# Attention softmax of a decoder layer: causal mask added by VectorE together with the row maximum, probability scale applied in two places, high half read in two halves

## The chip, the cores and the metric

One NeuronCore of a Trainium2 chip runs the whole decoder layer in one launch. The metric is device time in microseconds (us), from one launch to its end. The kernel before was timed three times: 1171.23 us is the median, 1167.91 and 1172.15 us are the ends. Engines: TensorE (PE) multiplies matrices into PSUM banks, VectorE (DVE), ScalarE (ACT) and GpSimd (POOL) work elementwise, SyncE (SP) issues DMAs. Each engine takes its own instructions in the order in which they are written; semaphores connect them.

## The reference, cut to what matters

A pre-norm decoder layer on `x` (4 x 512 x 512): latent attention with 16 heads and a causal mask, then an int8-like quantised linear layer pair, then a mixture of 8 experts with the best 2 per token. The change touches the attention's softmax alone.

```python
q = rmsnorm(x @ w_qa, q_norm_w) @ w_qb            # 16 heads, 128 plain + 64 rotary
kv = x @ w_kva                                    # 128 latent + 64 rotary (shared by the heads)
k_nope, v = split(rmsnorm(kv_c, kv_norm_w) @ w_kvb)
q_rope, k_rope = rotated by position (cos, sin)
scores = einsum('blhd,bmhd->bhlm', q, k) / sqrt(192)
scores = where(tril, scores, -1e30)
attn = softmax(scores, axis=-1)
out = einsum('bhlm,bmhd->blhd', attn, v).reshape(B, L, 2048) @ w_o
x = x + out                                       # x here went through a layer norm first
x = x + quantised_linear_pair(layernorm(x))       # scaled and rounded to +-127, silu gate between
x = x + mixture_of_experts(layernorm(x))
```

## The kernel before, in words

Everything that must be exact beyond fp16 is kept as two fp16 halves, a high one (the value rounded) and a low one (the rest), and a product of two such numbers is three matmuls (`TRI`).

After a preparation of the weights, `walk` goes over 32 steps `i`, each a pair of heads of one batch (4 batches x 8 pairs). All engines run the same `walk` with their own `pair` function; `j` is `i & 1`, so even and odd steps have different tables of extra work. In a step there are 8 slots `g`: two heads with four row blocks `k = g & 3` of 128 query rows, whose causal width is `n = 128 (k + 1)` columns. `G = 8 i + g` counts row blocks over the whole walk: 256 of them, 64 of each width (128, 256, 384, 512).

One row block passes these stations:

- PE `scores` (L1898 to L1903): five matmuls of width `n` into one of three score banks, and a sixth, 128 columns wide, which adds the mask (identity times `maskb`, with -1e30 above the diagonal) to the last 128 columns.
- DVE `row_max` (L1512): a reduction over the bank that gives the negated row maximum `NEGM`.
- POOL `bias` (L1059): `NB = NEGM * sc_exp`, one value a row.
- ACT `exps` (L1218): `exp(sc_exp * s + NB)` from the bank into `PF` in SBUF, with the row sum.
- DVE `row_scale`: the reciprocal of the sum (L1519) and its product with 4096, `R4` (L1521). `probs_hi` (L1529): the high half, `PF * R4` in fp16. `probs_lo` (L1536): the low half, `PF * R4` minus the high half.
- SP `turn_probs` (L1012): a DMA transposes both halves into `PT` (semaphore `pt_in[k]`). PE `values` (L1915) multiplies them with the latents once all four blocks of a head have landed.

DVE's `pair` issues in slot `g` first `row_max(g)` and then `row_scale`, `probs_hi` and `probs_lo` of `g - 1`. PE may be three row blocks ahead, since there are three score banks (`s_exp`).

Beside this, each step prepares the rotary part of the next one. PE `rope_mm(i+1)` (L1859, in even steps slot 4) is copied by ACT `rope_swap` in four pieces (L1237), POOL multiplies it with the sines (`rope_sin`, L1064), DVE multiplies the original with the cosines (`rotate`, L1556), POOL adds (`rope_sum`, L1070) and subtracts (`rope_split`, L1075), and ACT makes the halves (L1245, L1249). Even steps up to 22, twelve of them, also prepare one tile of the next batch (`prep`): ACT L1192 and L1194 (squares, after PE L1828), DVE L1474 and following, POOL `prep_norm` (L1053), and DVE `prep_split` (a cast L1495 and a subtraction L1497), on which PE `prep_t2` (L1837) waits in slot 6. The four even steps 24 to 30 have no such tile. Odd steps up to 21 do the layer norm of a tile ahead (DVE L1439 to L1449, POOL `prep_rstd` L1049). `nope_mm` (L1880) and `project` (L1930) are the other matmuls of a step.

In POOL's `pair`, slot `g` is `bias(g)` and then that slot's rotary part: in even steps `rope_sin` in slot 3, `rope_sum` in slot 5, `rope_split` in slot 6. `rope_sin` waits for `r_swap`, which ACT raises.

Of the kernel before, what the change touches and what calls it, by code (L numbers as in the profile page):

```python
# [17 lines left out]
B, L, D = 4, 512, 512  # L18
# [17 lines left out]
def decoder_layer(nc, x, fside, ctxw, w_qa, q_norm_w, w_qb, w_kva, kv_norm_w, w_kvb, w_o,  # L36
# [16 lines left out]
    with es:  # L53
# [3 lines left out]
        identf = es.enter_context(nc.sbuf_tensor("identf", [P, P], fp32))  # L57
        maskb = es.enter_context(nc.sbuf_tensor("maskb", [P, P], bf16))
        scal = es.enter_context(nc.sbuf_tensor("scal", [P, 40], fp32))
# [13 lines left out]
        qnw, knw = scal[:, 34:37], scal[:, 37:38]  # L73
        amaxq = scal[:, 31:34]

        ARENA = 52400
# [55 lines left out]
        small = take(40)  # L132
        NEGM, NB, SUM, RC, R4 = (small[:, 20 + 4 * k:24 + 4 * k] for k in range(5))
        rstd = small[:, 10:11]
# [122 lines left out]
        def ph_part(k, hl):  # L257

            return ph(k).rearrange("p (t l c) -> p t l c", l=2, c=P)[:, :, hl, :]
# [771 lines left out]
        def _(pool):  # L1031
            pool.memset(half, -0.5).then_inc(const_made, 1)
            pool.memset(phalf, 0.5).then_inc(const_made, 1)
            pool.memset(eone, math.e).then_inc(const_made, 1)
            for t, fill in ((ident16, 1.0), (identb, 1.0), (identf, 1.0)):
                pool.memset(t[:, :], 0.0).then_inc(const_made, 1)
            pool.memset(maskb[:, :], 0.0).then_inc(const_made, 1)
            pool.memset(KN[:, P + DR:2 * P + DR], 0.0).then_inc(const_made, 1)
            pool.wait_ge(const_made, 8)
            for t in (ident16, identb, identf):  # L1040
                pool.affine_select(out=t[:, :], in_=t[:, :], compare_op=ALU.not_equal, fill=1.0, base=0,
                                   pattern=[[-1, P]], channel_multiplier=1).then_inc(const_made, 1)

            pool.affine_select(out=maskb[:, :], in_=maskb[:, :], compare_op=ALU.is_ge, fill=-1e30, base=0,
                               pattern=[[-1, P]], channel_multiplier=1).then_inc(const_made, 1)
# [9 lines left out]
            def bias(G, g):  # L1055

                pool.wait_ge(s_max, G + 1)
                k = g & 3
                pool.tensor_tensor(NB[:, k:k + 1], NEGM[:, k:k + 1], sc_exp, ALU.mult).then_inc(s_bias, 1)  # L1059

# [16 lines left out]
            def pair(i, j, first=False, last=False, prep=None, ahead=None):  # L1077
                G = 8 * i
                for g in range(8):
                    bias(G + g, g)  # L1080
                    if (j, g) == (0, 2):
                        if prep is not None:
                            prep_norm(prep[0])
# [52 lines left out]
            rope_split(0, 0)  # L1136
            walk(pair)
            later_pool(pool)

# [223 lines left out]
        def _(dve):  # L1363
# [25 lines left out]
            def units_of_heads():  # L1389

                dve.wait_ge(amax_all, 2)
                own(dve.tensor_scalar(amx[:, 3:5], amx[:, 3:5], 1e-30, None, ALU.max))
                own(dve.reciprocal(ainv[:, 3:5], amx[:, 3:5]))
                own(dve.tensor_scalar(sc_exp, uk, amx[:, 3:4], 1.0 / math.sqrt(DN + DR), ALU.mult, ALU.mult))
                dve.tensor_scalar(sc_y, amx[:, 2:3], amx[:, 4:5], 1.0 / PSCALE, ALU.mult, ALU.mult).then_inc(units, 1)

# [111 lines left out]
            def row_max(G, g):  # L1508

                n = ((g & 3) + 1) * P  # L1510
                dve.wait_ge(s_mm, G + 1)
                dve.tensor_reduce(NEGM[:, (g & 3):(g & 3) + 1], banks[S_BANKS[G % 3]][:, 0:n], AX.X, ALU.max,  # L1512
                                  negate=True).then_inc(s_max, 1)

            def row_scale(G, g):

                k = g & 3
                dve.wait_ge(s_exp, G + 1)
                dve.reciprocal(RC[:, k:k + 1], SUM[:, k:k + 1]).then_inc(s_rc, 1)  # L1519
                dve.wait_ge(s_rc, G + 1)  # L1520
                dve.tensor_scalar(R4[:, k:k + 1], RC[:, k:k + 1], PSCALE, None, ALU.mult).then_inc(s_r4, 1)  # L1521

            def probs_hi(i, g):

                k, G = g & 3, 8 * i + g
                dve.wait_ge(s_r4, G + 1)
                if not (i == 0 and g < 4):
                    dve.wait_ge(pt_in[k], 16 * (2 * i + (g >> 2)))
                dve.tensor_scalar(ph_part(k, 0), pf(k).rearrange("p (t c) -> p t c", c=P), R4[:, k:k + 1], None,  # L1529
                                  ALU.mult).then_inc(s_hi, 1)  # L1530

            def probs_lo(G, g):

                k = g & 3
                dve.wait_ge(s_hi, G + 1)
                dve.scalar_tensor_tensor(out=ph_part(k, 1), in0=pf(k).rearrange("p (t c) -> p t c", c=P),  # L1536
                                         scalar=R4[:, k:k + 1], in1=ph_part(k, 0), op0=ALU.mult,
                                         op1=ALU.subtract).then_inc(s_lo, 1)
# [239 lines left out]
        def _(pe):  # L1778


            pe.wait_ge(const_made, 12)

# [103 lines left out]
            def scores(i, j, g):  # L1886
# [14 lines left out]
                pe.matmul(bank[:, 0:n], qr(j, h, q, P), kr(bp, 0, 0, n), start=False, stop=False)  # L1901
                pe.matmul(bank[:, 0:n], qr(j, 2, q, P), kr(bp, 1 + h, 0, n), start=False, stop=False)  # L1902
                pe.matmul(bank[:, q:n], identb[:, :], maskb[:, :], start=False, stop=True).then_inc(s_mm, 1)  # L1903

# [180 lines left out]
```

## Time and profile before

| what | before |
|---|---|
| device time, median of 3 (ends) | 1171.23 us (1167.91 to 1172.15) |
| span of the profiled execution | 1169.4 us |
| time around the span | not shown for this execution; the median lies 1.8 us above the span |
| PE busy | 980.4 us, 84% |
| DVE busy | 959.2 us, 82% |
| ACT busy | 678.1 us, 58% |
| POOL busy | 296.4 us, 25% |

The span is the time from the first to the last instruction. The walk lies at about 162 to 880 us; before it the weights are prepared, after it come the two later layers. Between 300 and 850 us the walk runs at the full clock of TensorE and repeats itself every two steps. The busy time of an engine adds its instructions' records; records of neighbours overlap a little, on PE a lot, so that for PE the distance from one start to the next is the cost of an instruction, not its own length.

### The profile page before, as it was taken

The page shows a single profiled execution, that of the slowest core. Times are in us where ns is not written, and L with a number is a line of the kernel's source. Part 1 is how long each engine was busy: PE and PEld are TensorE (multiplying, and loading weights), DVE is VectorE, ACT ScalarE, POOL GpSimd, SP SyncE. Part 2 cuts the span into 40 slices and gives each one's busy share as a digit, 9 for nine tenths or more (in the row PEclk, how much of TensorE's full clock was granted, in tenths as well). Part 3 has the DMA queues.
Part 4 walks back from the last instruction along what each step waited for, and adds up shares of the span by engine and source line. Part 5 has one row for each costly group of instructions (what it writes and reads, how often), then busy time and mean ns, then how long its engine had stood idle before and what let it go on. Part 6 is the DMA issues. An engine that isn't in the chain of part 4 may idle for free.

```text
span 1169.4 us, 18715 instructions
## 1 busy us (share of the span) xinstructions
PE 980.4 (84%) x6106; PEld 574.0 (49%) x6124; DVE 959.2 (82%) x2669; ACT 678.1 (58%) x1449; POOL 296.4 (25%) x524
## 2 busy tenths in 40 slices
PE   0446667899999999999999999999978655559997
PEld 0234444555555555555555555555545544435553
DVE  5757749989989888989998988888868898866885
ACT  1446557667667666756666666656512676754442
POOL 1036533223223223222322222213100113221211
PEclk9769779999999999999999999999989888769999
DMA  9300003433323336334335244336363520001333
GB/s 350 139 1 1 1 8 73 75 59 71 71 59 67 66 62 142 62 64 69 65 68 138 55 68 60 64 67 140 68 218 86 168 91 19 0 1 36 84 80 91
DMA packets 217328, 90.78 MB, mean 78 GB/s; under 512 B 191496, under 2 KB 202760, under 8 KB 216720
## 3 DMA queue, kind: packets, MB, share of 16 engines
q1 hardware_dynamic: 217232, 89.58, 33.5%
q8 instruction: 50, 0.82, 0.3%
q14 instruction: 46, 0.38, 0.1%
HBM read 36.06 MB, written 7.34 MB: 37 GB/s over the span
## 4 chain that ended last, share of the span: by engine, by line
PE 53%; DVE 30%; ACT 6%; issue 5%; POOL 3%; DMA 3%; SPq 0%; DVEq 0%; ACTq 0%; POOLq 0%
PE bank L1930 13%; PE bank L1880 8%; PE bank L1915 6%; PE bank L1828 3%; PE bank L1859 3%; DVE arena L709 2%; PE bank L1898 2%; DVE arena L711 2%; PE bank L1901 2%; PE bank L1899 2%; PE bank L1900 2%; PE bank L1902 2%; DVE arena L791 2%; DVE arena L675 2%; DVE arena L1529 2%
## 5 line engine op out<-in xcount | busy, mean ns | idle before, releaser
L1218 ACT ACTIVATE arena<-bank,arena,scal 128x128 f32<-128x128 f32 (+3 forms) x256 | 157.7, 616 | 112.7 <-POOL arena L1059 111.6
L1930 PE MATMUL bank<-arena 128*128 128x512 f16 x768 | 179.1, 381 | 1.9 <-DVE arena L1562 1.9
L1536 DVE SCALAR_TENSOR_TENSOR arena<-arena 128x128 f16<-128x128 f32 (+3 forms) x256 | 142.2, 555 | 9.1
L1059 POOL TENSOR_TENSOR arena<-arena,scal 128x1 f32<-128x1 f32 x256 | 51.7, 203 | 347.4 <-DVE arena L1512 345.7
L1880 PE MATMUL bank<-arena 128*128 128x512 f16 x576 | 137.6, 385 | 0.0
L1529 DVE TENSOR_SCALAR arena<-arena 128x128 f16<-128x128 f32 (+3 forms) x256 | 125.4, 490 | 7.4 <-DVE arena L1521 0.8
L1512 DVE TENSOR_REDUCE arena<-bank 128x1 f32<-128x128 f32 (+3 forms) x256 | 123.7, 483 | 7.8 <-PE bank L1903 6.7
L1915 PE MATMUL bank<-arena 128*128 128x512 f16 (+3 forms) x768 | 117.7, 304 | 11.5 <-DMA arena<-arena 5.8
L1930 PEld LDWEIGHTS bank<-arena 128*128 128x128 f16 x768 | 72.9, 98 | 81.0 <-issue 4.4
L1915 PEld LDWEIGHTS bank<-arena 128*128 128x128 f16 x768 | 71.8, 99 | 63.0 <-issue 16.5
L1237 ACT ACTIVATE arena<-bank 32x512 f32<-32x512 f32 x128 | 75.3, 588 | 26.0 <-PE bank L1859 24.7
L1898 PE MATMUL bank<-arena 128*128 128x128 f16 (+3 forms) x256 | 77.0, 301 | 9.1 <-DVE arena L1429 5.0
L1880 PEld LDWEIGHTS bank<-arena 128*128 128x128 f16 x576 | 54.4, 99 | 55.8 <-issue 3.5
L1249 ACT ACTIVATE arena<-arena 64x512 f16<-64x512 f32 x128 | 79.9, 624 | 1.2
L1902 PE MATMUL bank<-arena 128*128 128x128 f16 (+3 forms) x256 | 76.9, 300 | 0.0
L1900 PE MATMUL bank<-arena 128*128 128x128 f16 (+3 forms) x256 | 76.9, 300 | 0.0
L1901 PE MATMUL bank<-arena 128*128 128x128 f16 (+3 forms) x256 | 76.9, 300 | 0.0
L1899 PE MATMUL bank<-arena 128*128 128x128 f16 (+3 forms) x256 | 76.9, 300 | 0.0
L1228 ACT ACTIVATE arena<-bank 128x512 f16<-128x512 f32 x64 | 38.2, 596 | 65.8 <-PE bank L1880 65.5
L835 PE MATMUL bank<-identf,arena 128*128 128x128 f32 x192 | 37.7, 355 | 40.8 <-DVE arena L721 35.9
L1828 PE MATMUL bank<-arena 128*128 128x384 f16 (+1 forms) x384 | 54.8, 303 | 18.1 <-DVE arena L1386 15.7
L1064 POOL TENSOR_TENSOR arena<-arena 128x512 f32<-128x512 f32 x32 | 44.9, 1404 | 94.2 <-ACT arena L1237 94.1
(201 smaller groups left out, 2049.5 us busy)
## 6 DMA issues: line engine op xcount, KB each, us to landing
arena<-in_L_attn_w_qb SPq DMA_DIRECT2D x1, 4608.0 KB, 21.6
arena<-arena SPq DMA_TRANSPOSE x272, 2.7
arena<-in_x SPq DMA_DIRECT2D x4, 1024.0 KB, 6.9
arena<-in_L_attn_w_o SPq DMA_DIRECT2D x1, 4096.0 KB, 31.9
arena<-in_fside_BxS2xS SPq DMA_DIRECT2D x4, 1024.0 KB, 8.8
arena<-in_L_ffn_w SPq DMA_DIRECT2D x8, 512.0 KB, 7.6
out<-arena SPq DMA_DIRECT2D x16, 256.0 KB, 2.3
arena<-in_x SPq DMA_DIRECT2D x12, 256.0 KB, 3.0
```

The source lines that it names most:

```text
L1218: act.activation(pf(k), banks[S_BANKS[G % 3]][:, 0:n], ACT.Exp, bias=NB[:, k:k + 1], scale=sc_exp, accum_out=SUM[:, k:k + 1]).then_inc(s_e ...
L1512: dve.tensor_reduce(NEGM[:, (g & 3):(g & 3) + 1], banks[S_BANKS[G % 3]][:, 0:n], AX.X, ALU.max, negate=True).then_inc(s_max, 1)
L1529: dve.tensor_scalar(ph_part(k, 0), pf(k).rearrange("p (t c) -> p t c", c=P), R4[:, k:k + 1], None, ALU.mult).then_inc(s_hi, 1)
L1536: dve.scalar_tensor_tensor(out=ph_part(k, 1), in0=pf(k).rearrange("p (t c) -> p t c", c=P), scalar=R4[:, k:k + 1], in1=ph_part(k, 0), op0= ...
L1880: last = pe.matmul(banks[Q_BANK][:, :], wq(a, c, (i & 7) * 2 + h), ct(bp, b, c, 0, L), start=(k == 0), stop=(k == 3 * QC - 1))
L1898: pe.matmul(bank[:, 0:n], qn(h, 0, q, P), ct(bp, 0, QC, 0, n), start=True, stop=False)
L1899: pe.matmul(bank[:, 0:n], qn(h, 0, q, P), ct(bp, 1, QC, 0, n), start=False, stop=False)
L1900: pe.matmul(bank[:, 0:n], qn(h, 1, q, P), ct(bp, 0, QC, 0, n), start=False, stop=False)
L1901: pe.matmul(bank[:, 0:n], qr(j, h, q, P), kr(bp, 0, 0, n), start=False, stop=False)
L1902: pe.matmul(bank[:, 0:n], qr(j, 2, q, P), kr(bp, 1 + h, 0, n), start=False, stop=False)
L1915: last = pe.matmul(banks[O_BANK][:, kt * P:L], cn(bp, a, kt), pt(h, b, kt, kt * P, L - kt * P), start=(kt == 0 and n == 0), stop=(kt == TB ...
L1930: last = pe.matmul(banks[Y_BANK][:, :], ot(gp, a, k, (q & 3) * P, P), wo(b, gp * GH + k), start=(k == 0 and n == 0), stop=(k == GH - 1 and ...
```

## The change: mask, scale and halves

1. The mask matmul (L1903) is gone, and the fifth matmul ends the group. The mask is now `maskw`, 512 columns wide, zero except for the last 128. `row_max` is one `tensor_tensor_reduce` on DVE: it reads the bank and the last `n` columns of `maskw`, writes the sum back into the bank and gives the row maximum `ROWM`, not negated. The program has two instructions for it, the operation over the tile and one that writes the 128 x 1 result.
2. `bias` multiplies with `nsc_exp`, the negated `sc_exp` (one more small DVE instruction before the walk).
3. `row_scale` is the reciprocal alone. `probs_hi` takes the reciprocal as first scalar and 4096 as second. `R4`, which only `probs_lo` still reads, is made by POOL in a new function `row_unit`, placed right behind the next row block's `bias`; `probs_lo` waits for it (`s_r4`).
4. `probs_hi` reads and writes its columns as two halves of 64 in each block of 128 (`halves`), so the outermost size is 2 for each width.

```diff
@@ POOL, before the walk @@
-            pool.memset(maskb[:, :], 0.0).then_inc(const_made, 1)
+            pool.memset(maskw[:, :], 0.0).then_inc(const_made, 1)
-            pool.affine_select(out=maskb[:, :], in_=maskb[:, :], compare_op=ALU.is_ge, fill=-1e30, base=0,
+            pool.affine_select(out=maskw[:, L - P:L], in_=maskw[:, L - P:L], compare_op=ALU.is_ge, fill=-1e30, base=0,
                                pattern=[[-1, P]], channel_multiplier=1).then_inc(const_made, 1)
@@ POOL @@
-                pool.tensor_tensor(NB[:, k:k + 1], NEGM[:, k:k + 1], sc_exp, ALU.mult).then_inc(s_bias, 1)
+                pool.tensor_tensor(NB[:, k:k + 1], ROWM[:, k:k + 1], nsc_exp, ALU.mult).then_inc(s_bias, 1)
+
+            def row_unit(G, g):
+
+                k = g & 3
+                pool.wait_ge(s_rc, G + 1)
+                if G >= 4:
+                    pool.wait_ge(s_lo, G - 3)
+                pool.tensor_tensor(R4[:, k:k + 1], RC[:, k:k + 1], pscale, ALU.mult).then_inc(s_r4, 1)
@@ POOL, pair @@
                     bias(G + g, g)
+                    if not (first and g == 0):
+                        row_unit(G + g - 1, g - 1)
                     if (j, g) == (0, 2):
@@ DVE @@
-                dve.tensor_reduce(NEGM[:, (g & 3):(g & 3) + 1], banks[S_BANKS[G % 3]][:, 0:n], AX.X, ALU.max,
-                                  negate=True).then_inc(s_max, 1)
+                s = banks[S_BANKS[G % 3]][:, 0:n]
+                dve.tensor_tensor_reduce(out=s, in0=s, in1=maskw[:, L - n:L], scale=1.0, scalar=-3e38, op0=ALU.add,
+                                         op1=ALU.max, accum_out=ROWM[:, (g & 3):(g & 3) + 1]).then_inc(s_max, 1)
                 dve.reciprocal(RC[:, k:k + 1], SUM[:, k:k + 1]).then_inc(s_rc, 1)
-                dve.wait_ge(s_rc, G + 1)
-                dve.tensor_scalar(R4[:, k:k + 1], RC[:, k:k + 1], PSCALE, None, ALU.mult).then_inc(s_r4, 1)
+            def halves(v):
+
+                return v.rearrange("p t (h c) -> p h t c", h=2)
             def probs_hi(i, g):
-                dve.wait_ge(s_r4, G + 1)
+                dve.wait_ge(s_rc, G + 1)
-                dve.tensor_scalar(ph_part(k, 0), pf(k).rearrange("p (t c) -> p t c", c=P), R4[:, k:k + 1], None,
-                                  ALU.mult).then_inc(s_hi, 1)
+                dve.tensor_scalar(halves(ph_part(k, 0)), halves(pf(k).rearrange("p (t c) -> p t c", c=P)),
+                                  RC[:, k:k + 1], PSCALE, ALU.mult, ALU.mult).then_inc(s_hi, 1)
             def probs_lo(G, g):
                 dve.wait_ge(s_hi, G + 1)
+                dve.wait_ge(s_r4, G + 1)
@@ PE @@
-                pe.matmul(bank[:, 0:n], qr(j, 2, q, P), kr(bp, 1 + h, 0, n), start=False, stop=False)
-                pe.matmul(bank[:, q:n], identb[:, :], maskb[:, :], start=False, stop=True).then_inc(s_mm, 1)
+                pe.matmul(bank[:, 0:n], qr(j, 2, q, P), kr(bp, 1 + h, 0, n), start=False, stop=True).then_inc(s_mm, 1)
```

In a program order listing the first piece is POOL in an even step with a tile to prepare, from `prep_norm` (L1053) in slot 2 to `rope_sum` (L1070) in slot 5, before the change; L1064 is `rope_sin`, L1059 is `bias`.

```order
L1053 TENSOR_TENSOR arena<-arena,scal 128x2 [waits sv_made]
L1059 TENSOR_TENSOR arena<-arena,scal 128x1 [waits s_max]
L1064 TENSOR_TENSOR arena<-arena 128x512 [waits r_swap]
L1059 TENSOR_TENSOR arena<-arena,scal 128x1 [waits s_max] x2
L1070 TENSOR_TENSOR arena<-arena 128x512 [waits r_sin,r_rot]
```

The same place after the change; L1056 is `prep_norm`, L1062 `bias`, L1070 now `row_unit`, L1075 `rope_sin`, L1081 `rope_sum`.

```order
L1056 TENSOR_TENSOR arena<-arena,scal 128x2 [waits sv_made]
L1062 TENSOR_TENSOR arena<-arena,scal 128x1 [waits s_max]
L1070 TENSOR_TENSOR arena<-arena,scal 128x1 [waits s_lo,s_rc]
L1075 TENSOR_TENSOR arena<-arena 128x512 [waits r_swap]
L1062 TENSOR_TENSOR arena<-arena,scal 128x1 [waits s_max]
L1070 TENSOR_TENSOR arena<-arena,scal 128x1 [waits s_lo,s_rc]
L1062 TENSOR_TENSOR arena<-arena,scal 128x1 [waits s_max]
L1070 TENSOR_TENSOR arena<-arena,scal 128x1 [waits s_lo,s_rc]
L1081 TENSOR_TENSOR arena<-arena 128x512 [waits r_sin,r_rot]
```

Each `bias` now has a `row_unit` behind it, and the `row_unit` of slot 4 (row block 3) stands behind `rope_sin`.

The second piece is DVE in the same step, slot 4, before the change: `row_max(4)`, the two parts of `row_scale(3)`, `probs_hi(3)`, `probs_lo(3)`, `rotate` (L1556), `prep_split` (L1495, L1497).

```order
L1512 TENSOR_REDUCE arena<-bank 128x1 [waits s_mm]
L1519 RECIPROCAL arena<-arena 128x1 [waits s_exp]
L1521 TENSOR_SCALAR arena<-arena 128x1 [waits s_rc]
L1529 TENSOR_SCALAR arena<-arena 128x4x128 [waits pt_in3,s_r4]
L1536 SCALAR_TENSOR_TENSOR arena<-arena 128x4x128 [waits s_hi]
L1556 TENSOR_TENSOR arena<-bank,arena 128x512 [waits r_swap,r_split,r_mm]
L1495 CAST arena<-arena 128x512 [waits cn_made,ct_t,cf_made]
L1497 TENSOR_TENSOR arena<-arena 128x512 [waits ch_hi]
```

After the change (L1528 `row_max` in two instructions, L1535 reciprocal, L1547 `probs_hi`, L1555 `probs_lo`, L1575 `rotate`, L1510 and L1512 `prep_split`):

```order
L1528 ISA bank,arena<-bank,maskw 128x128 [waits s_mm]
L1528 ISA arena 128x1
L1535 RECIPROCAL arena<-arena 128x1 [waits s_exp]
L1547 TENSOR_SCALAR arena<-arena 128x2x4x64 [waits pt_in3,s_rc]
L1555 SCALAR_TENSOR_TENSOR arena<-arena 128x4x128 [waits s_r4,s_hi]
L1575 TENSOR_TENSOR arena<-bank,arena 128x512 [waits r_swap,r_split,r_mm]
L1510 CAST arena<-arena 128x512 [waits cn_made,ct_t,cf_made]
L1512 TENSOR_TENSOR arena<-arena 128x512 [waits ch_hi]
```

One small instruction is gone and one has come; `probs_lo` has a second semaphore, raised by POOL, and `rotate` and `prep_split` stand behind it as before.

## Rows read from the trace of the kernel before

**Rows 1.** 300-850 us: busy PE, PEld, DVE, ACT, POOL, clock; page's chain by engine.
```profile
300.00:850.00 550.00, 545.47 (x3478) 305.24 (x3476) 485.78 (x1352) 355.06 (x811) 143.44 (x294) 1.00 0.40 77
...
PE 53%; DVE 30%; ACT 6%; issue 5%; POOL 3%; DMA 3%; SPq 0%; DVEq 0%; ACTq 0%; POOLq 0%
```
**Rows 2.** Waits of PE, 300 to 850 us: who for whom, total, times, longest.
```profile
PE bank L1837 <- DVE arena L1497: 2.5, 9, 1.0
```
**Rows 3.** Instructions of PE in time: start, length, line, shape.
```profile
404.56 0.22 PE L1898 MATMUL bank<-arena 128*128 128x128 f16 x1
...
404.84 0.22 PE L1903 MATMUL bank<-maskb,identb 128*128 128x128 bf16 x1
404.90 0.38 PE L1930 MATMUL bank<-arena 128*128 128x512 f16 x1
```
**Rows 4.** Groups of DVE by form: count, busy us, mean ns, idle before.
```profile
L1521 DVE TENSOR_SCALAR arena<-arena 128x1 f32<-128x1 f32 x256 | 39.4, 154 | 8.8
L1529 DVE TENSOR_SCALAR arena<-arena 128x384 f16<-128x384 f32 x64 | 39.1, 611 | 1.9
L1512 DVE TENSOR_REDUCE arena<-bank 128x1 f32<-128x128 f32 x64 | 18.1, 283 | 1.0 <-PE bank L1903 1.0
L1512 DVE TENSOR_REDUCE arena<-bank 128x1 f32<-128x512 f32 x64 | 43.9, 686 | 4.3 <-PE bank L1903 3.4
L721 DVE SCALAR_TENSOR_TENSOR arena<-bank,arena 128x512 f32<-128x512 f32 x32 | 22.1, 745 | 4.2 <-PE bank L876 4.0
L1416 DVE SCALAR_TENSOR_TENSOR arena<-bank,scal,arena 128x128 f16<-128x128 f32 x32 | 9.6, 341 | 0.0
L1404 DVE SCALAR_TENSOR_TENSOR arena<-arena,scal 128x512 f16<-128x512 f32 x6 | 6.0, 1057 | 0.0
```
**Rows 5.** DVE in time, end of step 11 and step 12 (even, with a tile).
```profile
416.20 0.16 DVE L1519 RECIPROCAL arena<-arena 128x1 f32<-128x1 f32 x1 [0.94 <-ACT arena L1218]
...
435.04 0.22 DVE L1474 TENSOR_TENSOR arena<-bank,arena 128x64 f32<-128x64 f32 x1 [1.26 <-ACT arena L1194]
...
439.76 0.49 DVE L1529 TENSOR_SCALAR arena<-arena 128x512 f16<-128x512 f32 x1
440.28 0.75 DVE L1536 SCALAR_TENSOR_TENSOR arena<-arena 128x512 f16<-128x512 f32 x1
...
441.55 0.90 DVE L1495 CAST arena<-arena 128x512 f16<-128x512 f32 x1
442.49 0.69 DVE L1497 TENSOR_TENSOR arena<-arena 128x512 f16<-128x512 f32 x1
```
**Rows 6.** POOL in time, step 12, slots 3 and 4.
```profile
440.51 1.65 POOL L1064 TENSOR_TENSOR arena<-arena 128x512 f32<-128x512 f32 x1 [3.78 <-ACT arena L1237]
442.13 0.37 POOL L1059 TENSOR_TENSOR arena<-arena,scal 128x1 f32<-128x1 f32 x1
```
**Rows 7.** The wait chain before L1064, and PE in step 12.
```profile
438.05 2.39 ACT L1237 ACTIVATE arena<-bank 32x512 f32<-32x512 f32 x4 [0.41 <-PE bank L1859]
...
443.24 0.62 PE L1837 MATMUL bank<-ident,arena 128*128 128x128 f16 x8 [0.18 <-DVE arena L1497]
```
**Rows 8.** DVE and POOL at once: a read of SBUF through two ports, a small multiply.
```profile
196.85 0.49 DVE L1529 TENSOR_SCALAR arena<-arena 128x512 f16<-128x512 f32 x1
...
196.94 0.45 POOL L1059 TENSOR_TENSOR arena<-arena,scal 128x1 f32<-128x1 f32 x1
```
**Rows 9.** Step 28 (even, no tile): DVE, POOL, PE in time.
```profile
789.03 0.75 DVE L1536 SCALAR_TENSOR_TENSOR arena<-arena 128x512 f16<-128x512 f32 x1
...
790.12 1.27 POOL L1064 TENSOR_TENSOR arena<-arena 128x512 f32<-128x512 f32 x1 [3.39 <-ACT arena L1237]
791.34 0.34 POOL L1059 TENSOR_TENSOR arena<-arena,scal 128x1 f32<-128x1 f32 x2
...
793.48 1.79 PE L1915 MATMUL bank<-arena 128*128 128x512 f16 x12
```
**Rows 10.** Transposes of the probabilities at 789.8 us: issue to landing.
```profile
DMA to landing us min/median/max: 3.1/3.1/3.1
```

More of the change, by code:

```diff
@@ L57, in decoder_layer @@
         identf = es.enter_context(nc.sbuf_tensor("identf", [P, P], fp32))
-        maskb = es.enter_context(nc.sbuf_tensor("maskb", [P, P], bf16))
+        maskw = es.enter_context(nc.sbuf_tensor("maskw", [P, L], bf16))
         scal = es.enter_context(nc.sbuf_tensor("scal", [P, 40], fp32))
@@ L74, in decoder_layer @@
         amaxq = scal[:, 31:34]
+        nsc_exp = scal[:, 38:39]
+        pscale = scal[:, 39:40]
         ARENA = 52400
@@ L132, in decoder_layer @@
         small = take(40)
-        NEGM, NB, SUM, RC, R4 = (small[:, 20 + 4 * k:24 + 4 * k] for k in range(5))
+        ROWM, NB, SUM, RC, R4 = (small[:, 20 + 4 * k:24 + 4 * k] for k in range(5))
         rstd = small[:, 10:11]
@@ L1034, in _ @@
             pool.memset(eone, math.e).then_inc(const_made, 1)
+            pool.memset(pscale, PSCALE).then_inc(const_made, 1)
             for t, fill in ((ident16, 1.0), (identb, 1.0), (identf, 1.0)):
                 pool.memset(t[:, :], 0.0).then_inc(const_made, 1)
-            pool.memset(maskb[:, :], 0.0).then_inc(const_made, 1)
+            pool.memset(maskw[:, :], 0.0).then_inc(const_made, 1)
             pool.memset(KN[:, P + DR:2 * P + DR], 0.0).then_inc(const_made, 1)
-            pool.wait_ge(const_made, 8)
+            pool.wait_ge(const_made, 9)
             for t in (ident16, identb, identf):
@@ L1137, in _ @@
             walk(pair)
+            row_unit(8 * NPAIR - 1, 7)
             later_pool(pool)
@@ L1394, in units_of_heads @@
                 own(dve.tensor_scalar(sc_exp, uk, amx[:, 3:4], 1.0 / math.sqrt(DN + DR), ALU.mult, ALU.mult))
+                dve.tensor_scalar(nsc_exp, uk, amx[:, 3:4], -1.0 / math.sqrt(DN + DR), ALU.mult, ALU.mult)
                 dve.tensor_scalar(sc_y, amx[:, 2:3], amx[:, 4:5], 1.0 / PSCALE, ALU.mult, ALU.mult).then_inc(units, 1)
@@ L1778, in _ @@
         def _(pe):
-            pe.wait_ge(const_made, 12)
+            pe.wait_ge(const_made, 13)
             def transpose_head(h):
```

## The prediction

> **What bounds the kernel now.** I read the stretches first, then the chain, then who waits for whom, then single steps of the walk in order of time. From 300 to 850 us TensorE is busy 545.5 of 550 us at the full clock, VectorE 485.8 of 550 [rows 1]; more than half of the chain that ended last is TensorE's [rows 1]. In that stretch the longest entry of TensorE's waits is 2.5 us in total, for `prep_split` on VectorE [rows 2]. So the walk goes at TensorE's pace and repeats every two steps, and a matmul that goes is time gained, unless something else then comes late. VectorE is the next to look at: over two steps (44.65 us) it has pauses of 2.9 us in all beyond the usual gaps, the two long ones being 0.94 and 1.26 us [rows 5]. A change that loads VectorE or makes it wait has little room.
>
> **The mask matmul.** Six matmuls of 128 columns take from 404.56 to 404.90, 0.057 us each from start to start [rows 3]; the record's 0.22 us overlaps its neighbours. 256 of them: 14.6 us off TensorE. That is all the change can give while TensorE sets the pace. The score bank is also ready 0.06 us sooner, which matters to nobody.
>
> **The row maximum.** The reduction takes 686 ns at 512 columns and 283 at 128. An operation of VectorE on a bank and an SBUF tile with both as tensors takes 745 and 341 [rows 4], 59 more at either width. The second instruction, for the 128 x 1 result, has no row on VectorE; instructions of one column there last 154 ns [rows 4], and part of that overlaps its neighbour. I take 0.09 us, between 0 and 0.19 (a small one with a wait, below). Together +0.15 us a row block, from +0.06 to +0.25. That writing into a bank is dearer than writing into SBUF, no row shows; upper end: the 1057 ns of L1404 [rows 4] in place of 745, +0.31 us at 512 columns, +0.20 in the mean over the four widths. Below: if the sum did not slow the reduction at all, the +0.06 would go.
>
> **The scale.** L1521 goes from VectorE: it lasts 154 ns, and from its start to that of `probs_hi` I count 0.19 us, -0.19 a row block, 49 us over 256. Instead `probs_lo` waits for a small multiply of GpSimd. Rows 8 show what happens when such a multiply meets `probs_hi`: it starts at 196.94, 0.09 us after `probs_hi`, and lasts 0.45 us instead of 0.19, to 197.39, while `probs_hi` ends at 197.34. So the scale comes just after `probs_hi` ends, and `probs_lo` starts about 0.08 us later than now (0 if the multiply gets in first, 0.25 if all of its 0.19 us comes afterwards).
>
> **The halves.** At 384 columns, three blocks, `probs_hi` takes 611 ns, more than the 0.49 us at 512 [rows 4, 5]; with the outermost size 2 it should lie just below 0.49, at 0.41: -0.20 us, on 64 row blocks, 12.8 us off VectorE; 0 if it does not take.
>
> **VectorE in sum.** Over two steps (16 row blocks, 4 of them 384 wide): 16 x (-0.19 + 0.15 + 0.08) - 4 x 0.20 = -0.2 us. Away from what follows it stays as it is, and the 49 us are not gained anywhere: they were hidden behind TensorE.
>
> **What the wait on GpSimd costs.** `row_unit(3)` stands in GpSimd's queue behind `bias(4)`, and that behind `rope_sin(i+1)`. In even steps `rope_sin` waits for ScalarE's copies, which wait for `rope_mm` in slot 4 of TensorE: 438.05 us plus 2.39 us of copies, and L1064 starts at 440.51 [rows 6, 7]. None of this depends on VectorE. But `probs_lo(3)` is at 440.28 to 441.03 now [rows 5], before `rope_sin` has even begun. After the change:
> - `rope_sin` starts 0.06 us sooner (one mask matmul fewer between `scores(3)` and the copies), at 440.45. It lasts 1.27 us as in step 28 [rows 9], not the 1.65 of now [rows 6], since `probs_lo` no longer runs beside it: end 441.72. `bias(4)` 0.19, `row_unit(3)` 0.19, overlapping by 0.04 each: 442.02. `probs_lo(3)` starts about 442.09, 1.81 us later than now.
> - Behind it are `rotate` and `prep_split`. From `probs_lo(3)` to L1497 it is 2.21 us now [rows 5], of which the cast's 0.90 us is 0.4 too long because it stood beside `rope_sin`; with 0.49 it becomes 1.80. L1497 starts at 443.89 instead of 442.49: +1.40 us.
> - TensorE waits there already, 0.18 us before L1837 at 443.24 [rows 7]. So it starts 1.40 us later. The transposes of block 3 need 3.1 us [rows 10] from about 442.87, so `values` is ready at 446.0, before TensorE comes to it at 446.4: nothing on top.
> The loop is: TensorE's `scores(3)`, the chain above, L1837, and TensorE's own work to the next `scores(3)`, in which 13 of the 16 mask matmuls lie. Per two steps: +1.40 - 13 x 0.057 = +0.66 us. There are 12 even steps with a tile: +7.9 us.
>
> In the four even steps without a tile nobody waits for L1497, but for the probabilities. In step 28 `probs_lo(3)` runs 789.03 to 789.78; `rope_sin` ends at 791.39, `bias(4)` (with the next one, the record of two) starts at 791.34 [rows 9]. `row_max(3)`, 0.15 us longer, is here on the way to the copies, so all of that moves by 0.1: `row_unit(3)` ends at 791.79, `probs_lo(3)` at 792.6, and 3.1 us of transposes [rows 10] and an issue make 795.8. `values` starts at 793.48 now [rows 9]: +2.3 us, less 12 x 0.057 = 0.7: +1.6 us, four times, +6.5 us.
>
> In odd steps `rope_mm` is a slot earlier, `rope_sin` is over before the reciprocal of block 3 (416.20 [rows 5]), and I count at most 0.2 us on VectorE for `rope_sum` before `row_unit(4)`; it has the 1.26 us to lose it in. Its wait for the rest over two steps is 1.8 - 0.4 (the cast) - 0.2 + 0.3 (`prep_rstd` behind a `row_unit`) = +1.5 us, against 2.9 us of standing still plus 0.7 of longer period. It fits, not by much.
>
> **Sum.** +7.9 + 6.5 = +14.4 us on the profiled execution's span of 1169.4: 1183.8. The median of the runs is 1.8 us above that span; I add the same: 1185.6 us, slower by 1.2%. The mask matmuls' 14.6 us are in it: the waits alone cost 29 us.
>
> **The skill against the rows.** The small multiply held up beside `probs_hi`, and the cast held up beside `rope_sin` [rows 5, 8], are one effect. The Trainium skill, "SBUF — State Buffer", section "Who interferes with whom", says that a VectorE instruction in a two-port mode or with two SBUF inputs and a GpSimd instruction exclude each other for the whole instruction, whoever is first. By that rule, the trace agrees, and it speaks against the third part of the change: the 384-wide `probs_hi` joins those that lock GpSimd out; in the sum it changes the 0.08 us, not the 1.8.
>
> **The rivals.**
> - *VectorE becomes the bound (slower still).* For: only about 2 us of two steps remain. It needs the combined operation at the upper end, +0.20 us more a row block, 3.2 us over 16; beyond the room of 2.1 that is 1.1 us over two steps, 16 times, +18 us: 1203. Against: 745 ns stands for 32 like operations, 1057 for six with strided input [rows 4]. The Trainium skill, "Vector Engine (DVE) Microarchitecture Reference", section "Points that are easy to get wrong", says that such three-operand forms run at half rate with two non-bf16 SBUF sources; here one source is a bank and the mask is bf16, so by its words it does not apply, and no run here shows it. Were the rate halved all the same, then at (745 - 341) / 384 = 1.05 ns a column [rows 4] the 2560 columns of a step would add 2.7 us, over two steps 5.4 against a room of 2.1: some 50 us in all; I give it 0.03 of this rival's chance.
> - *Faster.* The wait is absorbed. The price on TensorE is paid only if the late `probs_lo(3)` reaches L1837 or `values`. If VectorE caught it up, all of 14.6 us would show: 1156.6. The point from which it decides is the wait at L1837: below 0.7 us more than now the change gains. For: VectorE gets 49 and 13 us lighter in instructions. Against: the 1.8 us arise after VectorE has done all it can; being earlier there only makes the wait longer.
> - *No difference.* Half of the wait: if the chain `bias(4)`, `row_unit(3)`, `probs_lo(3)` is shorter by 0.7 us, or the steps without a tile have more room at `values` than I count; about 1171.
> - *The halves do not take:* +0.8 us on VectorE over two steps, inside its room; 1186 stays.
>
> **Chances.** Forecast (with the last rival) 0.62, VectorE as bound 0.16, no difference 0.09, faster 0.13. The likeliest one's own range is 1178 to 1194: 0.5 us either way at each of 16 waits. The range for 8 in 10 goes to 1203 above, and below to 1172. About 0.5%, 5.9 us, can be told from no change here; so: slower 0.77, same 0.10, faster 0.13.
>
> **What would show it.** Right: no L1903, TensorE's busy time down; in even steps `probs_lo(3)` waits about 1.8 to 2.5 us for GpSimd's new multiply, and none elsewhere waits over 0.3; TensorE's wait at the tile's second transposes grows from 0.18 to about 2 us, and in steps 24 to 30 it waits for the transposes of probabilities; 384-wide `probs_hi` near 0.41 us; the period of two steps 45.3 instead of 44.65 us. Wrong: TensorE's waits as short as now; or VectorE without pauses and TensorE waiting in odd steps too, then the combined operation is dearer than 745 ns.

## The result, and the profile after

| | before | after |
|---|---|---|
| median (ends), 4 runs each | 1170.52 us (1167.91 to 1172.15) | 1193.28 us (1191.62 to 1196.38) |
| ratio after / before | | 1.0199, 95% interval 1.0181 to 1.0217 |
| span of the profiled execution | 1169.4 us | 1194.6 us |

The change costs 22.8 us. The forecast was 1185.6 us, in a range from 1172 to 1203. The kernel before has a fourth time here, 1169.81 us, so its median is 1170.52 and not the 1171.23 of three. The profiled execution of the kernel after is the longest of its four (1196.38 us), so the two spans differ by 25.2 us; the walk itself, from its first to its last reciprocal on VectorE, took 712.8 us (167.16 to 880.00) against 690.8 (165.15 to 855.95), 22.0 more. The same stretch as in [rows 1] (busy PE, PEld, DVE, ACT, POOL, clock) and the page's chain:

```profile
300.00:850.00 550.00, 525.40 (x3191) 286.36 (x3189) 441.65 (x1319) 345.89 (x785) 173.11 (x479) 0.99 0.37 75
...
PE 44%; issue 20%; DVE 18%; POOL 10%; ACT 5%; DMA 2%; SPq 0%; POOLq 0%; DVEq 0%; ACTq 0%
```

TensorE was busy 545.5 us there and VectorE 485.8; now TensorE has 24.6 us of pauses in 550, VectorE 108. Who waits, in that stretch, first for TensorE, then one entry of VectorE's list (total us, times, longest):

```profile
PE bank L1856 <- DVE arena L1512: 15.2, 9, 1.7
PE bank L1933 <- DMA arena<-arena: 7.7, 3, 2.6
...
DVE arena L1555 <- POOL arena L1070: 42.1, 69, 3.3
```

L1856 is `prep_t2`, L1512 the end of `prep_split`: 2.5 us in [rows 2], now 15.2. L1933 is `values`, L1555 `probs_lo`, L1070 `row_unit`.

**Step 12, with a tile.** VectorE, GpSimd and TensorE in time; the counterparts are [rows 5 to 7].

```profile
446.82 0.48 DVE L1547 TENSOR_SCALAR arena<-arena 128x512 f16<-128x512 f32 x1
449.58 0.75 DVE L1555 SCALAR_TENSOR_TENSOR arena<-arena 128x512 f16<-128x512 f32 x1 [2.28 <-POOL arena L1070]
...
450.85 0.42 DVE L1510 CAST arena<-arena 128x512 f16<-128x512 f32 x1
451.30 0.69 DVE L1512 TENSOR_TENSOR arena<-arena 128x512 f16<-128x512 f32 x1
```
```profile
402.54 1.26 POOL L1075 TENSOR_TENSOR arena<-arena 128x512 f32<-128x512 f32 x1 [3.40 <-ACT arena L1251]
...
447.92 1.26 POOL L1075 TENSOR_TENSOR arena<-arena 128x512 f32<-128x512 f32 x1 [3.40 <-ACT arena L1251]
449.14 0.19 POOL L1062 TENSOR_TENSOR arena<-arena,scal 128x1 f32<-128x1 f32 x1
449.29 0.19 POOL L1070 TENSOR_TENSOR arena<-arena,scal 128x1 f32<-128x1 f32 x1
```
```profile
452.05 0.62 PE L1856 MATMUL bank<-ident,arena 128*128 128x128 f16 x8 [1.69 <-DVE arena L1512]
```

Read it as a chain: `rope_sin` (L1075) ends at 449.18, `bias` and `row_unit` follow, and `probs_lo`, which could have run at 447.3, starts at 449.58. `prep_split` ends 2.4 us after that and TensorE, which was at the place at 450.4, starts at 452.05. From one `rope_sin` to that of the next pair of steps it is 447.92 - 402.54 = 45.38 us. Before, it was 440.51 [rows 6] less the start in this row, 44.65 us:

```profile
395.86 1.66 POOL L1064 TENSOR_TENSOR arena<-arena 128x512 f32<-128x512 f32 x1 [3.78 <-ACT arena L1237]
```

**Step 28, without a tile**; counterparts in [rows 9].

```profile
808.71 0.75 DVE L1555 SCALAR_TENSOR_TENSOR arena<-arena 128x512 f16<-128x512 f32 x1 [3.25 <-POOL arena L1070]
```
```profile
762.81 1.26 POOL L1075 TENSOR_TENSOR arena<-arena 128x512 f32<-128x512 f32 x1 [3.13 <-ACT arena L1251]
...
807.05 1.26 POOL L1075 TENSOR_TENSOR arena<-arena 128x512 f32<-128x512 f32 x1 [3.13 <-ACT arena L1251]
```
```profile
812.91 2.70 PE L1933 MATMUL bank<-arena 128*128 128x512 f16 x12 [2.56 <-DMA arena<-arena]
815.40 3.56 PE L1948 MATMUL bank<-arena 128*128 128x512 f16 x12
818.80 0.22 PE L1917 MATMUL bank<-arena 128*128 128x128 f16 x1
```

TensorE waits 2.56 us for the transposes, and then something comes that the prediction does not have: the twelve matmuls of `values` last 2.70 us where they lasted 1.79 [rows 9]. The stretches from 806 us on (same columns as above) show the granted clock:

```profile
806.00:812.90 6.90, 4.09 (x20) 1.62 (x19) 4.16 (x9) 3.93 (x10) 3.10 (x6) 1.00 0.47 117
812.90:815.40 2.50, 2.49 (x12) 1.47 (x13) 2.31 (x6) 2.44 (x5) 1.49 (x3) 0.64 0.90 298
815.40:818.80 3.40, 3.40 (x14) 1.40 (x13) 1.85 (x6) 1.92 (x5) 0.45 (x2) 0.76 0.22 45
818.80:822.00 3.20, 3.20 (x22) 1.84 (x21) 2.52 (x9) 0.55 (x2) 0.51 (x2) 1.00 0.28 55
```

The granted clock is given as a share of the full 2.4 GHz; 0.64 and 0.76 are means over stretches in which it stood partly at its lower level, 1.2 GHz. The period is 807.05 - 762.81 = 44.24 us; before, the same distance is 790.12 [rows 9] less the start in this row, 40.61 us:

```profile
749.51 1.26 POOL L1064 TENSOR_TENSOR arena<-arena 128x512 f32<-128x512 f32 x1 [3.39 <-ACT arena L1237]
```

**What VectorE's instructions cost now**, by form in the same 550 us:

```profile
L1528 DVE CUSTOM_DVE_ANT_0 bank<-bank,maskw 128x512 f32<-128x512 f32 x49 | 33.9, 693 | 1.4 <-PE bank L1921 1.2
L1528 DVE DVE_READ_ACCUMULATOR2_ANT arena<- 128x1 f32 x196 | 27.6, 141 | 0.0
L1547 DVE TENSOR_SCALAR arena<-arena 128x384 f16<-128x384 f32 x49 | 20.7, 422 | 1.7
```

The combined mask and maximum takes 693 ns at 512 columns, the reduction took 686 [rows 4]. And the second instruction costs nothing that can be seen:

```profile
802.64 0.69 DVE L1528 CUSTOM_DVE_ANT_0 bank<-bank,maskw 128x512 f32<-128x512 f32 x1
803.25 0.14 DVE L1528 DVE_READ_ACCUMULATOR2_ANT arena<- 128x1 f32 x1
803.25 0.16 DVE L1535 RECIPROCAL arena<-arena 128x1 f32<-128x1 f32 x1
803.45 0.42 DVE L1547 TENSOR_SCALAR arena<-arena 128x384 f16<-128x384 f32 x1
804.02 0.62 DVE L1555 SCALAR_TENSOR_TENSOR arena<-arena 128x384 f16<-128x384 f32 x1
```

It starts together with the reciprocal, 0.61 us after the operation; before, a reciprocal also started 0.61 us after a reduction of 512 columns (435.77 to 436.38). The last two rows show the everyday price of `row_unit`: 0.15 us between `probs_hi` and `probs_lo`, against 0.03 before (439.76 + 0.49 to 440.28 in [rows 5]).

### The profile page after: what moved, and what is told of

The parts are those of the page before. It is cut to its first block, busy times and chain, and to the rows that moved or that the text cites. A ratio compares the mean times of both kernels' runs of the same rounds, so it can differ in the third digit from the quotient of the medians.

```text
span 1194.6 us, 18987 instructions
## 1 busy us (share of the span) xinstructions
PE 986.6 (83%) x5868; PEld 566.4 (47%) x5868; DVE 918.8 (77%) x2670; ACT 679.6 (57%) x1449; POOL 340.6 (29%) x781
## 4 chain that ended last, share of the span: by engine, by line
PE 44%; issue 20%; DVE 18%; POOL 10%; ACT 5%; DMA 2%; SPq 0%; POOLq 0%; DVEq 0%; ACTq 0%
PE bank L1948 9%; PE bank L935 5%; PE bank L1899 5%; PE bank L1847 4%; PE bank L1933 4%; POOL arena L1075 2%; DVE arena L711 2%; PE bank L944 2%; DVE arena L713 2%; POOL arena L1070 2%; PE bank L1878 2%; POOL arena L1062 2%; DVE arena L677 1%; DVE arena L723 1%; PE bank L1917 1%
## 5 line engine op out<-in xcount | busy, mean ns | idle before, releaser
L1555 DVE SCALAR_TENSOR_TENSOR arena<-arena 128x128 f16<-128x128 f32 (+3 forms) x256 | 145.2, 567 | 72.3 <-POOL arena L1070 55.9
L1948 PE MATMUL bank<-arena 128*128 128x512 f16 x768 | 181.1, 384 | 1.9 <-DVE arena L1581 1.9
L1062 POOL TENSOR_TENSOR arena<-arena,scal 128x1 f32<-128x1 f32 x256 | 51.0, 199 | 341.5 <-DVE arena L1528 338.9
L1933 PE MATMUL bank<-arena 128*128 128x512 f16 (+3 forms) x768 | 123.6, 314 | 21.9 <-DMA arena<-arena 15.5
L1528 DVE CUSTOM_DVE_ANT_0 bank<-bank,maskw 128x128 f32<-128x128 f32 (+3 forms) x256 | 125.8, 491 | 15.1 <-PE bank L1921 14.8
L1899 PE MATMUL bank<-arena 128*128 128x512 f16 x576 | 137.3, 384 | 0.0
L1547 DVE TENSOR_SCALAR arena<-arena 128x128 f16<-128x128 f32 (+3 forms) x256 | 121.6, 475 | 8.0 <-DVE arena L1535 0.3
L1948 PEld LDWEIGHTS bank<-arena 128*128 128x128 f16 x768 | 74.4, 99 | 83.4 <-issue 7.0
L1933 PEld LDWEIGHTS bank<-arena 128*128 128x128 f16 x768 | 74.5, 102 | 82.1 <-issue 35.6
L1899 PEld LDWEIGHTS bank<-arena 128*128 128x128 f16 x576 | 57.0, 99 | 56.1 <-issue 2.7
L1878 PE MATMUL bank<-arena 128*128 128x512 f16 x288 | 67.4, 379 | 0.0
```

What stands on the lines that cost most here:

```text
L1528: dve.tensor_tensor_reduce(out=s, in0=s, in1=maskw[:, L - n:L], scale=1.0, scalar=-3e38, op0=ALU.add, op1=ALU.max, accum_out=ROWM[:, (g & ...
L1547: dve.tensor_scalar(halves(ph_part(k, 0)), halves(pf(k).rearrange("p (t c) -> p t c", c=P)), RC[:, k:k + 1], PSCALE, ALU.mult, ALU.mult).t ...
L1878: last = pe.matmul(banks[R_BANK][:, :], wr(b, c, i & 7), ct(bp, a, c, 0, L), start=(k == 0), stop=(k == 3 * QC - 1))
L1899: last = pe.matmul(banks[Q_BANK][:, :], wq(a, c, (i & 7) * 2 + h), ct(bp, b, c, 0, L), start=(k == 0), stop=(k == 3 * QC - 1))
L1933: last = pe.matmul(banks[O_BANK][:, kt * P:L], cn(bp, a, kt), pt(h, b, kt, kt * P, L - kt * P), start=(kt == 0 and n == 0), stop=(kt == TB ...
L1948: last = pe.matmul(banks[Y_BANK][:, :], ot(gp, a, k, (q & 3) * P, P), wo(b, gp * GH + k), start=(k == 0 and n == 0), stop=(k == GH - 1 and ...
```

## The experiments

Ratios are against runs of the kernel before on the same chip; its medians there were 1170.01 us (e1 to e4) and 1170.25 us (e5 to e8). Where two experiments come from different chips, the difference of their ratios is the better measure.

**e1: `rope_sin` behind `row_unit(3)`.** One line of the changed kernel:

```diff
@@ POOL, pair @@
-                    if (j, g) == (0, 3):
+                    if (j, g) == (0, 4):
                         if not last:
                             rope_sin(i + 1)
```

> The changed kernel with one call moved: in even steps rope_sin stands in GpSimd's slot 4, behind bias(4) and row_unit(3), instead of slot 3. My theory, the multiply with the sines in front of row_unit(3): rope_sin starts when ScalarE's copies are done in any case, so nothing becomes later; probs_lo(3) waits under 0.3 us instead of 2.3 to 3.3, TensorE's waits go, and the mask matmuls' 14.6 us show: 1155 to 1160 us, period of two steps 43.7 instead of 45.4. Rival A, the wait is the port shared with GpSimd, whatever the order: 1190 or more. Rival B, the combined mask and maximum on VectorE is what costs: 1185 or more.

Measured: 1154.91 us, ratio 0.9872 (0.9844 to 0.9901), 0.1 us under the expected range. The same entry of VectorE's waits (total, times, longest), and `probs_lo(3)` of step 12; then all that is listed of TensorE's waits from 300 to 850 us:

```profile
DVE arena L1555 <- POOL arena L1070: 11.7, 55, 0.3
```
```profile
434.53 0.49 DVE L1547 TENSOR_SCALAR arena<-arena 128x512 f16<-128x512 f32 x1
435.17 0.75 DVE L1555 SCALAR_TENSOR_TENSOR arena<-arena 128x512 f16<-128x512 f32 x1
```
```profile
PE bank L1933 <- DMA arena<-arena: 5.3, 1, 5.3
PE bank L1847 <- DVE arena L1581: 0.9, 1, 0.9
```

The longest wait of `probs_lo` is 0.3 instead of 3.3 us. No wait of TensorE at `prep_t2` (L1856) is listed any more; the 5.3 us are one wait behind 820 us, at the end of the walk, and the whole walk of the kernel before has one of 5.4 us at the same instruction. The period is 43.72 us in steps with a tile and 39.47 in those without. One call in another slot is worth 38 us, from 2.0% slower to 1.3% faster than before. Rival A falls: GpSimd and VectorE have the same instructions as in the changed kernel, only the order is different. Rival B falls: the combined operation is in this kernel.

**e2: R4 back on VectorE**, the rest as changed.

```diff
@@ DVE, row_scale @@
                 dve.reciprocal(RC[:, k:k + 1], SUM[:, k:k + 1]).then_inc(s_rc, 1)
+                dve.wait_ge(s_rc, G + 1)
+                dve.tensor_scalar(R4[:, k:k + 1], RC[:, k:k + 1], PSCALE, None, ALU.mult).then_inc(s_r4, 1)
@@ POOL, pair @@
-                    if not (first and g == 0):
-                        row_unit(G + g - 1, g - 1)
```

> The changed kernel with the product R4 back on VectorE, right behind the reciprocal; mask and halves as changed. My theory: no instruction of VectorE waits for row_unit any more, VectorE carries 49 us more but hides it: 1155 to 1160 us. Rival A (VectorE was near its limit and needs the relief): 1165 to 1175. Rival B (the combined mask and maximum costs): 1185 or more.

Measured: 1154.28 us, 0.9868 (0.9840 to 0.9897), 0.7 us under the expected range. Without the wait on GpSimd the loss is gone. VectorE has 256 more instructions than in e1 and the kernel is as fast, so giving them to GpSimd brought nothing: from the reciprocal of row block 3 in step 12 to its `probs_lo` it is 0.80 us here (434.06 to 434.86) and 0.84 in e1 (434.33 to 435.17), where the wait for GpSimd takes back what the instruction saved.

**e3: the scale alone** on the kernel before: `row_unit` in POOL's `pair` as in the change, `RC` and 4096 as scalars of `probs_hi`, no L1521; the mask matmul and the whole blocks stay.

> The kernel before with the third part of the change alone: GpSimd makes R4 in row_unit, probs_hi takes the reciprocal and 4096; mask matmul and whole blocks as before. My theory: all the loss is here, some 2 us at each of 12 steps with a tile less the 0.2 that TensorE waits already, and 4.2 us (2.5 of waiting and 1.7 of lower clock) at each of 4 without: 1200 to 1212 us, slower than the whole change. Rival B (the mask part costs): 1171 to 1175.

Measured: 1199.41 us, 1.0262 (1.0230 to 1.0294), 0.6 us under the forecast's lower end. Its waits:

```profile
PE bank L1849 <- DVE arena L1510: 14.3, 9, 1.6
PE bank L1927 <- DMA arena<-arena: 7.5, 3, 2.5
...
DVE arena L1548 <- POOL arena L1069: 45.3, 94, 3.2
```

They are those of the whole change. This part alone is slower than the four together.

**e4: the mask alone** on the kernel before: `tensor_tensor_reduce` and `nsc_exp` as in the change, no L1903.

> The kernel before with the mask on VectorE alone: tensor_tensor_reduce, no mask matmul, negated factor in bias; R4 and probs_hi as before. My theory: TensorE gives back 14.6 us, VectorE has room for the 0.08 us a row block that the accumulator read costs: 1155 to 1160 us. Rival B (the combined operation or its write into the bank delays the score banks): 1171 or more.

Measured: 1167.24 us, 0.9971 (0.9955 to 0.9986). My theory missed: 3 us came, not 14.6. Rival B's 1171 did not come either, and the combined operation is as short here as in the whole change (694 ns at 512 columns). TensorE's waits from 300 to 850 us tell why (before, [rows 2] had 2.5 us as the longest entry):

```profile
PE bank L1855 <- DVE arena L1509: 3.5, 9, 0.4
PE bank L1846 <- DVE arena L1580: 2.3, 7, 1.4
PE bank L1916 <- ACT arena L1229: 1.7, 4, 0.7
```

TensorE comes earlier and finds VectorE, which has not become faster, not ready: at `prep_t2` (L1855), at the bank that `add_y` (L1580) empties, and at a score bank. The period in steps with a tile falls to 44.30 us, 0.35 less, where 16 mask matmuls are worth 0.91.

**e5: the pause filled.** In the steps without a tile ten matmuls whose result nobody uses go in front of `values(i, 0)`.

```diff
@@ PE, pair of the changed kernel @@
                     if (j, g) == (0, 7):
+                        if prep is None:
+                            for _ in range(10):
+                                pe.matmul(banks[P_BANK][:, :], wq(0, 0, 0), ct(1, 0, 0, 0, L), start=True, stop=True)
                         values(i, 0)
```

> The changed kernel with ten extra matmuls of 512 columns (2.2 us of work, results used by nobody) on TensorE in the steps 24, 26, 28 and 30, in front of values(i, 0), where it stands still 2.6 us for the transposes. Theory, the lower clock: after the pause the granted clock is 0.64 and then 0.76, and 24 matmuls take 1.7 us more than at full clock; with the pause filled the clock stays at 1 and 4 x 1.7 = 6.8 us come back: 1186 to 1188 us. Rival: those matmuls are slow because of the transfers that run at the same time: no gain, 1193 or more.

Measured: 1185.82 us, 1.0139 (1.0121 to 1.0158), 7.5 us under the changed kernel (7.0 by the ratios) and 0.2 under the expected range. TensorE in step 28, two stretches (columns as above), and `rope_sin` of steps 26 and 28:

```profile
804.60 2.32 PE L1982 MATMUL bank<-arena 128*128 128x512 f16 x10
807.35 1.79 PE L1933 MATMUL bank<-arena 128*128 128x512 f16 x12 [0.43 <-DMA arena<-arena]
808.97 2.75 PE L1948 MATMUL bank<-arena 128*128 128x512 f16 x12
```
```profile
807.30:809.00 1.70, 1.65 (x13) 1.10 (x14) 1.51 (x5) 1.67 (x4) 1.42 (x3) 1.00 1.04 378
809.00:811.50 2.50, 2.50 (x15) 1.15 (x13) 2.31 (x7) 1.94 (x4) 0.52 (x3) 1.00 0.47 94
```
```profile
758.85 1.27 POOL L1075 TENSOR_TENSOR arena<-arena 128x512 f32<-128x512 f32 x1 [3.14 <-ACT arena L1251]
...
801.45 1.27 POOL L1075 TENSOR_TENSOR arena<-arena 128x512 f32<-128x512 f32 x1 [3.14 <-ACT arena L1251]
```

The clock stays at 1, `values` lasts 1.79 us again although the transfers run beside it as before (DMA share 1.04), and the period is 42.60 instead of 44.24 us: 1.64 us of lower clock a period. The two groups of matmuls say the same: 2.70 and 3.56 us against 1.79 and 2.75, 1.72 in all. The transposes come as late as before; only what the lower clock added behind them goes.

**e6: the halves alone** on the kernel before.

```diff
@@ DVE, probs_hi @@
-                dve.tensor_scalar(ph_part(k, 0), pf(k).rearrange("p (t c) -> p t c", c=P), R4[:, k:k + 1], None,
-                                  ALU.mult).then_inc(s_hi, 1)
+                dve.tensor_scalar(halves(ph_part(k, 0)), halves(pf(k).rearrange("p (t c) -> p t c", c=P)),
+                                  R4[:, k:k + 1], None, ALU.mult).then_inc(s_hi, 1)
```

> The kernel before with the halves alone (the fourth part). probs_hi at 384 columns 0.42 us instead of 0.61. Theory: VectorE was hidden behind TensorE, so its 12 us are worth at most the 0.2 us that TensorE waits at the tile's second transposes in 12 steps: 1168 to 1171 us, no change that can be told. Rival (VectorE set the pace in part): 1160 or less.

Measured: 1165.93 us, 0.9960 (0.9947 to 0.9974). Neither: 4.3 us are twice what the 0.2 us at `prep_t2` give, and far from the rival's 10. At `prep_t2`, where [rows 2] has 2.5 us, 0.2 are left:

```profile
PE bank L1841 <- DVE arena L1497: 0.2, 1, 0.2
```

That is 2.3 us in this stretch, and it shows in the period with a tile, 44.47 us instead of 44.65. Where the other 2 us come from was not separated. In the profiled executions, one of each kernel, 1.26 us of them lie in the period from step 12 (47.00 and 45.74 us), where VectorE waited 3.53 us for the DMA of `in_x` before and at most 2.7 in e6; that this is the doing of the halves is not shown.

**e7: mask and halves**, R4 on VectorE and read by `probs_hi` as before (e4 and e6 together).

> Mask and halves together on the kernel before, R4 on VectorE and read by probs_hi. The mask alone gave 3 us, mask, halves and the first scalar together gave 16. Theory: with the mask alone TensorE is early and waits for VectorE at the second transposes and at project's bank (add_y); the 0.2 us of the halves in each 384-wide row block remove those waits: 1154 to 1158 us. Rival (it was probs_hi's wait for R4 that cost): 1165 to 1168.

Measured: 1159.89 us, 0.9910 (0.9891 to 0.9929). Between the two expectations. The halves give 7.4 us on top of the mask (e4; 7.1 by the ratios), more than their 4.3 alone. TensorE waits more for VectorE there: at `prep_t2` its waits are 3.5 us with the mask alone and 1.8 here. The 5.6 us to e2 (4.9 by the ratios, whose intervals just overlap; in the profiled executions the period goes from 43.91 to 43.56 us) are the first scalar, the only difference: here `probs_hi` waits for R4, in e2 only for the reciprocal. VectorE in step 12, first e7 and then e2, R4 and `probs_hi`:

```profile
435.30 0.15 DVE L1534 TENSOR_SCALAR arena<-arena 128x1 f32<-128x1 f32 x1
435.49 0.49 DVE L1546 TENSOR_SCALAR arena<-arena 128x512 f16<-128x512 f32 x1
```
```profile
434.25 0.15 DVE L1534 TENSOR_SCALAR arena<-arena 128x1 f32<-128x1 f32 x1
434.34 0.48 DVE L1546 TENSOR_SCALAR arena<-arena 128x512 f16<-128x512 f32 x1
```

It is 0.19 us from start to start where `probs_hi` waits for the instruction right before it, and 0.09 where it waits only for the one before that: 0.10 us a row block.

**e8: both mends**, e2 and e1's moved call.

> The changed kernel with R4 back on VectorE and rope_sin in slot 4 of the even steps, the two mends together. With R4 on VectorE steps 24 to 30 had periods of 40.0 us, with rope_sin late 39.4, and 43.6 against 43.7 in the steps before. Theory: bias(4) no longer stands behind rope_sin, which gives the 0.6 us of the four last pairs of steps: 1151 to 1154 us. Rival (the two mends remove the same wait): 1154 to 1156.

Measured: 1150.94 us, 0.9836 (0.9819 to 0.9853), better than both kernels: 19.3 us under the kernel before on the same chip. That is 0.06 us under the expected range. The theory holds: the last pairs of steps take 39.4 us as in e1 (`rope_sin` at 731.73 and 771.14), not 40.0 as in e2 (734.73 and 774.76), because `bias(4)` no longer stands behind `rope_sin` either.

## Why the prediction was right, and where its sizes were off

- *The mechanism.* `row_unit(3)` behind `bias(4)` behind `rope_sin`, `probs_lo(3)` behind `row_unit(3)`, and TensorE behind that at two different places. All of it is in the trace, and e1 shows the cause by moving `rope_sin` alone. That move also frees `bias(4)`; e2, which leaves `bias(4)` where it is and takes only `probs_lo`'s wait away, wins back the same 38 us.
- *Steps with a tile.* Forecast +0.66 us a period, 45.3 us; measured 45.38 against 44.65, +0.73. The wait of `probs_lo(3)` is 2.28 us by the profile's count from `probs_hi`'s end; `probs_hi` was 0.35 us earlier relative to `rope_sin` than before, as VectorE's own work had shrunk. From the first reciprocal of step 0 to that of step 24, over the twelve, it is 542.6 against 534.5 us: +8.1, forecast +7.9.
- *Steps without a tile: the term that was mis-sized.* Forecast +1.6 us each; measured +3.6 (44.24 against 40.61). The wait at `values` came out as 2.56 us, forecast 2.3. What was missing are the 1.64 us of lower clock behind it (e5), 6.6 us over four periods. The prediction took each matmul at full clock and did not ask what TensorE's own pause does to it. With this term the sum of 14.4 becomes 21 us, and 22.8 were measured. The 3.6 us of a period add up: TensorE stands still 2.83 us where it did not before (2.56 at `values`, 0.26 at the `scores` that need `exps(4)`'s bank), the lower clock costs 1.7, and 16 mask matmuls give back 0.9. From the first reciprocal of step 24 to the last of the walk it is 170.2 against 156.2 us: +14.0, forecast +6.5.
- *The row maximum.* +0.15 us a row block was taken, about +0.02 is measured (0.01 for the operation, the accumulator read hidden beside the reciprocal). 0.06 came from a scalar_tensor_tensor as the nearest row; the reduction it replaces was the better neighbour. Its two lower bounds, 0 for either part, had it. In the sum it was worth only the 0.1 us that moved the chain in each of the four steps without a tile, but it took the first rival's ground away: VectorE had pauses of 108 us in 550. The half rate that this rival priced is not there: from 128 to 512 columns the combined operation goes from 292 to 693 ns, 1.04 ns a column, and the reduction from 283 to 686 [rows 4], 1.05. `probs_lo` reads two SBUF tiles, one fp32 and one fp16, and takes 751 ns at 512 columns, as long as the 745 of the form with one source in a bank [rows 4].
- *GpSimd's small multiply.* 0.08 us between `probs_hi` and `probs_lo` were taken; 0.15 against 0.03 were measured, +0.12. It lasts 0.19 us where nothing is beside it and 0.3 beside `probs_hi`:

```profile
803.61 0.31 POOL L1070 TENSOR_TENSOR arena<-arena,scal 128x1 f32<-128x1 f32 x1
```

  It ends at 803.92, 0.05 us after `probs_hi`. The Trainium skill, "SBUF — State Buffer", section "Who interferes with whom", has the two exclude each other for the whole instruction; the trace agrees. The `probs_hi` beside it is the 384-wide form, in two halves now and 422 ns long (0.41 forecast).
- *"They were hidden behind TensorE": wrong as a general statement.* The prediction gave VectorE's savings no worth. e6 shows 4.3 us for the halves alone, e4 that the mask matmuls alone give 3 of their 14.6 us, and e7 against e2 that 0.10 us a row block is worth about 5 us. TensorE's 2.5 us of waits in 550 [rows 2] told how much it waited, not how near VectorE was behind it at the three places.
- *The signs.* `probs_lo(3)` waits 2.28 us in steps with a tile, inside the forecast 1.8 to 2.5, but 3.25 in those without; elsewhere from 300 to 850 us 0.31 at most. TensorE's wait at `prep_t2` is 1.69 us (the sum had 0.18 + 1.40). TensorE's busy time, which was to go down, did not: the page has 986.6 us against 980.4. In the walk it fell only from 675.1 us (163 to 861) to 671.6 (165 to 885), partly since the matmuls behind the pauses last longer, and behind the walk the mean granted clock was lower in this execution (0.85 from 885 us on, 0.87 from 861 us on before); why is open.
- *Luck.* The measured 1193.3 us lies just inside the forecast's own 1178 to 1194. That range allowed 0.5 us either way at each of 16 waits; the miss was 0.07 us a period at twelve of them and 2.0 at four. So the range held without this miss having been foreseen.
- *The parts.* Scale 1.0262, mask 0.9971, halves 0.9960, mask and halves 0.9910, all without the queueing 0.9872 (e1). The whole, 1.0199, is e1's kernel plus one badly placed call: 38.3 us by the ratios.

## What to carry to other kernels

Before a small operation goes to an engine with room, read what stands in front of it in that engine's queue and what those instructions wait for: that GpSimd was busy 25% of the time said nothing here, the 3.8 us wait ahead in its queue decided. When a wait is added to TensorE, add the clock behind it as a term of its own. And where one engine is busy 99%, its own saving is paid out only as far as the second engine can follow; take both from the same step.

## What the runs showed of the hardware

- After a pause of 2.56 us, following 0.26 us at 809.10, TensorE's granted clock was 0.64 for 2.5 us and 0.76 for the next 3.4; after a pause of 1.69 us in step 12 it stayed at 1:

```profile
452.00:453.70 1.70, 1.65 (x16) 1.02 (x16) 1.70 (x5) 0.66 (x2) 1.23 (x3) 1.00 1.01 148
```

  The Trainium skill, "TensorE: Matmul & The Clock Gate", section "Part 1: The HAM clock gate (the "warmup" mystery)", says that the low level is the default and activity releases it; the return to 1.00 at 818.80 agrees, and e5 shows that useless matmuls hold it.
- An add with a maximum over a bank, written back into the bank, took 693 ns at 512 columns against 686 for the maximum alone, and the read of its accumulator ran beside the next instruction.
- On VectorE an instruction started 0.19 us after a one-column instruction whose result it waited for, and 0.09 us after it where it waited only for the one before that (e7 and e2).
- A one-column multiply of GpSimd took 0.19 us alone and 0.31 us beside a 422 ns `probs_hi` of VectorE, ending 0.05 us after it.
